# A decoder layer on one core: self attention's normalised rows are turned by VectorE and a DRAM round trip, the last tile's probabilities by TensorE, and two groups of loads are asked for by ScalarE's queue

## The chip, the cores and the metric

The kernel runs on one core of a Trainium2 chip. Its time is the device time of one execution in microseconds (us). TensorE is written PE in the profile, VectorE DVE, ScalarE ACT, GpSimd POOL, and SyncE SP; PEld is TensorE's loading of weights, which lies beside its matmuls.

## The reference, cut to what matters

A pre-norm decoder layer over x of 4 x 1024 rows of 512 numbers, in float32. Three parts are added to x one after the other: a self attention against 2048 given keys and values, a cross attention of 16 heads over 1601 context rows, and a mixture of experts. The change is in the first part alone:

```
def _L0_attn_ref(q, k, v, scale_factor, dropout_p):
    b, s, d = q.shape                      # 4, 1024, 512
    step = s // 4
    scale = q[:, ::step].reshape(b, -1)    # 4 normalised rows of a batch: 2048 numbers, one for each key
    qk = jnp.einsum('bsd,btd->bst', q, k)  # against 2048 keys
    scaled_qk = qk * scale[:, None, :]
    softmax_qk = jax.nn.softmax(scaled_qk, axis=-1)
    return jnp.einsum('bst,btv->bsv', softmax_qk, v)

x = x + _L0_attn_ref(_layernorm(x, axis=-1), L0_attn_k, L0_attn_v, L0_attn_scale_factor, L0_attn_dropout_p)
```

## The kernel before, in words

`self_attention` (line 97) writes one instruction stream for each engine by hand; semaphores order them, and no scheduler moves anything. It works on 32 tiles of 128 rows. Every number that goes into a matmul is split into a high and a low part, and a product is three matmuls of 512 columns (`matmul3`: lines 47 to 49, high by high, high by low, low by high). For tile t:

- VectorE makes the normalised rows (`normalize`, `sa_normed`, L498). Rows lie on partitions, but a matmul wants the 512 numbers of a row on partitions, so TensorE turns them by four 128x128 transposes (`turn`, `sa_nT_ps`, L322). ScalarE copies the high part (`high_n`, L417) and VectorE makes the low part (`low_n`, L503).
- TensorE scores the tile against four groups of 512 keys (`score`, 48 matmuls). VectorE multiplies by the scale (`scale_block`, L515; the trace calls the buffer `rows`, since it is a part of the `rows` tensor of the next stage), finds the maximum (`row_max`, L519), ScalarE takes the exponential (`exp`, L422).
- The probabilities have to be turned as well. VectorE turns all 32x32 squares in one instruction (`turn_p`, L523), SyncE sends the result to the DRAM tensor `turned_p` (L223), waits until it is there, and reads it back in four pieces, which puts the squares in their places (`move`, L226). ScalarE makes the high part (`high_p`, L430), GpSimd the low part (`low_p`, L291).
- TensorE weighs the values (`weigh`, 48 matmuls into `sa_o_ps`), and VectorE adds (`add`, L540).

TensorE's stream for tile t is: the scores of tile t+1, the turn of tile t+2, the weighing of tile t. So a tile's probabilities have one weighing and one scoring of other tiles to get through exponential, turning, DRAM and splitting. The exponential of tile t+1 writes the buffer from which `low_p(t)` reads, and waits for it. Tile 0's probabilities are turned by TensorE (`turn_first_p`, L348), as nothing is there to cover a trip.

The scale rows of the batches (1 MB each, `load_scale`, L219) and the three weights of the next stage (1 MB each, L255) are asked for by SyncE in its own order. The weights are turned by TensorE (`turn_last`, L373, into the banks of the scores, with ScalarE L439 and VectorE L575 splitting them) with three groups of context rows: 15 groups, nine of them before the last tile's weighing, one behind each quarter of it, and three at its end. The next stage begins with L878.

## Time and profile before

| | |
|---|---|
| median of 3 runs | 3819.49 us (3815.13 to 3820.21) |
| the profiled execution | 3817.16 us, of which the span is 3815.3 us |
| granted TensorE clock, mean | 0.993 |
| TensorE, VectorE, ScalarE, GpSimd busy | 98%, 63%, 38%, 44% |
| self attention | from the start to 769.67 us |

How to read it: times are microseconds from the span's start. "Busy" counts instructions from start to end; as TensorE's matmuls overlap (a row says 0.39 us where the next begins 0.23 us later), the distance between two starts says what a matmul costs, and its duration does not. A row of the timeline is: start, length of the row in us, engine, line, operation, what it writes <- what it reads, shape, count; in brackets the idle time of the engine before it and what ended it. PEclk is the granted TensorE clock as a share of 2.4 GHz. SPq rows are DMAs as SyncE asks for them.

### The profile page before, as it was taken

The numbers are of one execution on the slowest core, as the hardware profiler recorded it, in microseconds if no ns is written. First come the engines' busy times: TensorE is split into PE (matmuls) and PEld (weight loads), VectorE is DVE, ScalarE is ACT, GpSimd is POOL, SyncE is SP. The second block draws the span as 40 slices with busy tenths as digits, with TensorE's granted clock in tenths as the row PEclk, the third lists the DMA queues.
The fourth block names the chain that finished last, engine by engine and source line by source line (L and its number), as shares of the span: only waits on it lengthen the run. The fifth ranks groups of instructions, "written<-read, shape, count | busy, mean of one in ns | idle before, by whom it ended". The sixth has DMA issues, their size and how long they took to land. (4 is left out here: it accounts for less than half of the span.)

```text
span 3815.3 us, 62978 instructions
## 1 busy us (share of the span) xinstructions
PE 3730.7 (98%) x18664; PEld 2480.3 (65%) x18665; DVE 2386.6 (63%) x6129; ACT 1434.0 (38%) x1793; POOL 1687.6 (44%) x984
## 2 busy tenths in 40 slices
PE   8999999999988999999999999999999999999998
PEld 7888888788876544444444444454444777777886
DVE  6544444344466888888888888888888543434235
ACT  3222222222333455545555455545555221222332
POOL 2222222200023776677666766676665222312334
PEclk9999999999999999999999999999999999999999
DMA  6444444555565122222211222222211434327679
GB/s 203 125 128 131 134 121 121 162 199 187 180 196 180 36 58 58 58 56 58 58 29 34 58 58 59 58 56 58 48 31 40 157 123 138 111 89 257 213 279 340
DMA packets 245485, 446.75 MB, mean 117 GB/s; under 512 B 20024, under 2 KB 104536, under 8 KB 241244
## 3 DMA queue, kind: packets, MB, share of 16 engines
q1 hardware_dynamic: 215196, 366.37, 33.3%
q0 software_dynamic: 14752, 49.29, 3.6%
q10 hardware_dynamic: 15264, 27.79, 1.9%
q8 instruction: 130, 2.13, 0.2%
q14 instruction: 143, 1.17, 0.1%
HBM read 262.21 MB, written 181.17 MB: 116 GB/s over the span
## 5 line engine op out<-in xcount | busy, mean ns | idle before, releaser
L1165 DVE CUSTOM_DVE_ANT_0 xf_unread<-xa_mx_ps,mask_q 128x402 bf16<-128x402 f32 x1984 | 1033.7, 574 | 279.0 <-PE xa_mx_ps L1158 152.8
L1788 ACT ACTIVATE probs<-xa_scores 128x1024 f32<-128x1024 f32 (+1 forms) x416 | 417.5, 1024 | 417.6 <-PE xa_scores L1662 411.5
L1788 ACT ACTIVATE xa_probs<-xa_scores 128x1024 f32<-128x1024 f32 (+1 forms) x416 | 417.3, 1024 | 387.0 <-PE xa_scores L1662 387.0
L1662 PE MATMUL xa_scores<-mask_t,ident_b 128*128 128x512 bf16 (+1 forms) x1664 | 549.4, 388 | 0.0
L1623 POOL TENSOR_TENSOR xa_sums<-xa_sums,xa_probs 128x1024 f32<-128x1024 f32 x220 | 519.6, 2383 | 18.1 <-POOL xa_sums L1623 15.9
L1623 POOL TENSOR_TENSOR xa_sums<-xa_sums,probs 128x1024 f32<-128x1024 f32 x220 | 519.4, 2380 | 18.1 <-POOL xa_sums L1623 14.6
L1158 PE MATMUL xa_mx_ps<-xa_kp,queries 96*128 96x402 f32 x1024 | 364.7, 418 | 0.0
L1158 PE MATMUL xa_mx_ps<-xf_kp,queries 96*128 96x402 f32 x960 | 342.1, 418 | 0.0
L1656 PE MATMUL xa_scores<-queries,xf_kp 97*128 97x512 f32 (+1 forms) x832 | 284.7, 423 | 15.1 <-ACTq L1810 8.3
L1158 PEld LDWEIGHTS xa_mx_ps<-xa_kp,queries 96*128 96x128 f32 x1024 | 181.7, 189 | 169.4 <-DVE xf_maxima L1165 107.8
L1656 PE MATMUL xa_scores<-queries,xa_kp 97*128 97x512 f32 (+1 forms) x832 | 284.5, 423 | 1.8 <-ACT probs L1788 1.8
L1662 PEld LDWEIGHTS xa_scores<-mask_t,ident_b 128*128 128x128 bf16 (+1 forms) x1664 | 122.9, 100 | 244.5 <-issue 211.8
L1158 PEld LDWEIGHTS xa_mx_ps<-xf_kp,queries 96*128 96x128 f32 x960 | 170.3, 189 | 159.6 <-DVE xf_maxima L1165 102.2
L291 POOL TENSOR_TENSOR sa_pT_low<-rows,sa_pT_high 128x512 fp32r<-128x512 f32 x124 | 156.9, 1299 | 186.0 <-ACT sa_pT_high L430 186.0
L430 ACT ACTIVATE sa_pT_high<-rows 128x512 fp32r<-128x512 f32 x124 | 68.1, 621 | 406.2 <-DMA rows<-turned_p 406.2
L47 PE MATMUL sa_o_ps<-sa_v_high,sa_pT_high 128*128 128x512 f32 x512 | 203.7, 398 | 7.7 <-POOL sa_pT_low L291 7.3
L49 PE MATMUL sa_scores<-weights,sa_nT_low 128*128 128x512 f32 x512 | 204.3, 399 | 0.0
L47 PE MATMUL sa_scores<-weights,sa_nT_high 128*128 128x512 f32 x512 | 202.5, 395 | 1.4 <-DVE sa_nT_low L503 1.4
L48 PE MATMUL sa_scores<-queries,sa_nT_high 128*128 128x512 f32 x512 | 202.7, 396 | 0.0
L1656 PEld LDWEIGHTS xa_scores<-queries,xf_kp 97*128 97x128 f32 (+1 forms) x832 | 148.9, 187 | 82.4 <-ACT xa_probs L1788 26.0
L49 PE MATMUL sa_o_ps<-sa_v_high,sa_pT_low 128*128 128x512 f32 x512 | 200.3, 391 | 0.0
L48 PE MATMUL sa_o_ps<-sa_v_low,sa_pT_high 128*128 128x512 f32 x512 | 200.1, 391 | 0.0
(418 smaller groups left out, 7258.4 us busy)
## 6 DMA issues: line engine op xcount, KB each, us to landing
turned_p<-rows SPq DMA_DIRECT2D x31, 1024.0 KB, 3.8
rows<-turned_p SPq DMA_DIRECT2D x124, 256.0 KB, 4.6
bridge_rows<-sorted_in SPq DMA_DIRECT2D x78, 256.0 KB, 3.3
sorted_out<-ex_made ACTq DMA_DIRECT2D x78, 256.0 KB, 4.3
queries<-qT_high SPq DMA_DIRECT2D x30, 512.0 KB
xf_kp<-kT_high SPq DMA_DIRECT2D x16, 800.5 KB, 11.8
xa_kp<-kT_high SPq DMA_DIRECT2D x16, 800.5 KB
rows<-in_ctx SPq DMA_DIRECT2D x16, 768.0 KB, 4.8
```

Source lines behind the costliest of these rows:

```text
L47: pe.matmul(out, lh, rh, start=start, stop=False)
L48: pe.matmul(out, lh, rl, start=False, stop=False)
L49: return pe.matmul(out, ll, rh, start=False, stop=stop)
L291: pool.tensor_tensor(pT[1][:, mine, :].rearrange("p c (i q) -> p c i q", q=SQUARE), raw_pT[:, mine, :, :], words(pT[0][:, mine, :]).rearra ...
L430: act.activation(pT[0][:, mine, :].rearrange("p c (i q) -> p c i q", q=SQUARE), raw_pT[:, mine, :, :], ACT.Copy).then_inc(pT_high, 1)
L1158: return pe.matmul(out[:, 0:MKEYS], qp[0:MAXROW, j, first:first + P], kp[0:MAXROW, j, MFIRST[kb]:MFIRST[kb] + MKEYS], start=True, stop=True)
L1165: return dve.tensor_tensor_reduce(out=unread[slot % 2][:, :], in0=scores[:, 0:MKEYS], in1=mask_q[:, half * QB + qt, MFIRST[kb]:MFIRST[kb] ...
L1623: pool.tensor_tensor(sums[pr][:, :, :], left[pr][:, :, :], right[pr][:, :, :], ALU.add).then_inc(pool_added, 1)
L1656: pe.matmul(scores[pr][0:keys, jj, :], kp[par][0:ROWS97, j, kt * P:kt * P + keys], qp[par][0:ROWS97, j, queries], start=True, stop=False)
L1662: last = pe.matmul(scores[pr][0:keys, jj, :], ident_b[0:keys, 0:keys], mask_t[0:keys, kt, queries], start=False, stop=True)
L1788: act.activation(prob[ring][pr][0:keys, :, :], scores[pr][0:keys, :, :], ACT.Exp, scale=SCALE).then_inc(exped, 1)
```

## The change

Rows are turned in another way for tiles 2 to 31. VectorE turns the 32x32 squares of the normalised rows (`turn_n`, into `sa_spare`), SyncE sends them to a new DRAM tensor `turned_n` and reads them back in four pieces into `sa_normed` (`move_n`); ScalarE (`high_moved_n`) and VectorE (`low_moved_n`) split them from there. In the tile, both now stand behind the exponential and behind the turning of the probabilities. TensorE no longer turns rows in the tiles' loop. The last tile's probabilities are turned by TensorE, as the first tile's (`turn_end_p`), and the groups of `turn_last` are spread over its weighing, three behind each quarter. The scales of batches 1 to 3 and the three weights are asked for by ScalarE, one in each of tiles 0 to 2 and 26 to 28, behind that tile's exponential.

```
+                def move_n(t):
+                    sp.wait_ge(turned, t + 3)
+                    sp.dma_start(turned_n, spare[:, :]).then_inc(n_out, 16)
+                    sp.wait_ge(n_out, 16 * (t - 1))
+                    for a in range(QB):
+                        sp.dma_start(normed[a * SQUARE:(a + 1) * SQUARE, :].rearrange("k (i n) -> k i n", n=P),
+                                     turned_n[:, a * P:(a + 1) * P].rearrange("(i k) n -> k i n", k=SQUARE)).then_inc(n_in, 16)
...
-                load_scale(1)
-                for t in range(2):
-                    if t > 0:
+                def ask(t):
+                    if not (isinstance(t, int) and t == 0):
                         load_add(t)
                         store(t - 1)
                     load_norm(t + 3)
+                    move_n(t + 2)
                     move(t + 1)
-                    load_scale(t + 2)
...
-                sp.wait_ge(scaled_to, NB * (tiles - S // P) + NB + 1)
-                for w, weight in enumerate(weights):
-                    sp.dma_start(scale[:, w, :, :], weight.rearrange("(r p) n -> p r n", p=P)).then_inc(weights_in[w], 16)
...
                 def tile(t, ahead):
-                    first = isinstance(t, int) and t == 0
-                    for j in range(NB) if ahead >= 1 else ():
-                        if first and j == NB - 1:
-                            turn_first_p(0)
-                            turn_first_p(1)
+                    ends = isinstance(t, int) and t in (0, tiles - 1)
+                    for j in range(NB - 1) if ahead >= 1 else ():
                         score(t + 1, j)
-                    if ahead >= 2:
-                        turn(t + 2)
-                    for n in range(AHEAD) if ahead == 0 else ():
-                        turn_last(n)
+                    for j in range(2) if ends else ():
+                        turn_end_p(t, j)
+                    if ahead >= 1:
+                        score(t + 1, NB - 1)
                     for j in range(NB):
                         weigh(t, j)
-                        if first and j + 2 < NB:
-                            turn_first_p(j + 2)
-                        if ahead == 0 and AHEAD + j < GROUPS_W:
-                            turn_last(AHEAD + j)
+                        if ends and j + 2 < NB:
+                            turn_end_p(t, j + 2)
+                        for n in range(FULL) if ahead == 0 else ():
+                            turn_last(FULL * j + n)
...
+                def high_moved_n(t):
+                    act.wait_ge(scored, NB * t)
+                    act.wait_ge(n_in, 16 * QB * (t - 1))
+                    act.activation(nT[0][:, :, :].rearrange("p c (i r) -> p c i r", r=SQUARE), raw_nT,
+                                   ACT.Copy).then_inc(nT_high, 1)
+
...
+                def load_weight(w):
+                    act.wait_ge(scaled_to, NB * (tiles - S // P) + NB + 1)
+                    act.dma_start(scale[:, w, :, :],
+                                  weights[w].rearrange("(r p) n -> p r n", p=P)).then_inc(weights_in[w], 16)
...
                     if ahead >= 1:
                         exp(t + 1)
+                    if isinstance(t, int) and t < B - 1:
+                        if t == 0:
+                            wait_v_split(act)
+                        load_scale(t + 1)
+                    if isinstance(t, int) and 0 <= t - WEIGHTS_FROM < len(weights):
+                        load_weight(t - WEIGHTS_FROM)
+                    if ahead >= 2:
+                        high_moved_n(t + 2)
...
+                def turn_n(t):
+                    dve.wait_ge(normal, t + 3)
+                    if isinstance(t, int) and t == 2:
+                        dve.wait_ge(v_low_pool, POOL_V)
+                    else:
+                        dve.wait_ge(n_out, 16 * (t - 2))
+                    dve.transpose(n_squares, normed_by_row).then_inc(turned, 1)
+
...
                     invert(t)
                     if ahead >= 2:
                         normalize(t + 2)
+                        turn_n(t + 2)
...
+                    for j in range(2, NB) if ends else ():
+                        low_end_p(t, j)
+                        for n in range(FULL) if ahead == 0 else ():
+                            low_last(FULL * (j - 2) + n)
+                    if ahead >= 1 and not (isinstance(t, int) and t + 1 == tiles - 1):
+                        turn_p(t + 1)
                     if ahead >= 2:
-                        low_n(t + 2)
+                        low_moved_n(t + 2)
```

On VectorE the loop over tiles read so before, from the tile's rows being normalised (L498) to the sum of the tile before (L540):

```order
L498 TENSOR_SCALAR sa_normed<-sa_x_norm,sa_mean_var,sa_rstd 128x512
L515 TENSOR_TENSOR rows<-sa_scores,sa_scale 128x512
...
L519 TENSOR_REDUCE sa_neg_max<-rows 128x1
L503 TENSOR_TENSOR sa_nT_low<-sa_nT_ps,sa_nT_high 128x512
L523 STREAM_TRANSPOSE rows<-rows 128x2048
L540 SCALAR_TENSOR_TENSOR sa_out<-sa_o_ps,sa_inv_total,sa_x_add 128x512
```

The same place of the changed kernel (its lines are numbered anew):

```order
L525 TENSOR_SCALAR sa_normed<-sa_x_norm,sa_mean_var,sa_rstd 128x512
L534 STREAM_TRANSPOSE sa_spare<-sa_normed 128x512
L556 TENSOR_TENSOR rows<-sa_scores,sa_scale 128x512
...
L560 TENSOR_REDUCE sa_neg_max<-rows 128x1
L564 STREAM_TRANSPOSE rows<-rows 128x2048
L542 TENSOR_TENSOR sa_nT_low<-sa_normed,sa_nT_high 128x512
L581 SCALAR_TENSOR_TENSOR sa_out<-sa_o_ps,sa_inv_total,sa_x_add 128x512
```

A transpose of 128x512 has come in ahead of the first scaling, and the low part of the rows has gone behind the turning of the probabilities. SyncE's queue in the same loop is now:

```order
L208 DMA sa_x_add<-in_x 128x512
L212 DMA x<-sa_out 128x512
...
L204 DMA sa_x_norm<-in_x 128x512
L232 DMA turned_n<-sa_spare 128x512
L235 DMA sa_normed<-turned_n 32x4x128 x4
...
L224 DMA turned_p<-rows 128x2048
L227 DMA rows<-turned_p 32x4x512 x4
```

L232 and L235 are new; the others stand in the order that they had.

## Rows read from the trace of the kernel before

**Rows 1.** The page: busy time of each engine.

```profile
PE 3730.7 (98%) x18664; PEld 2480.3 (65%) x18665; DVE 2386.6 (63%) x6129; ACT 1434.0 (38%) x1793; POOL 1687.6 (44%) x984
```

**Rows 2.** Stretches: us, then each engine's busy time, PEclk, DMA share, GB/s.

```profile
0.00:769.67 769.67, 747.61 (x3341) 609.76 (x3342) 379.53 (x510) 183.80 (x272) 191.19 (x180) 0.99 0.46 140
...
70.00:75.00 5.00, 3.41 (x17) 2.63 (x16) 3.59 (x4) 2.67 (x5) 2.97 (x3) 1.00 1.04 357
...
750.00:752.00 2.00, 2.00 (x7) 1.52 (x6) 0.00 (x0) 0.00 (x0) 2.00 (x2) 0.50 0.00 0
```

**Rows 3.** Waits of TensorE to 770 us: in total, times, longest.

```profile
PE sa_o_ps L47 <- POOL sa_pT_low L291: 7.3, 2, 5.7
...
PE cxl_banks L878 <- SPq L843: 3.3, 1, 3.3
```

**Rows 4.** Timeline of TensorE, the last loop tile and the tile behind the loop.

```profile
693.31 0.40 PE L47 MATMUL sa_scores<-weights,sa_nT_high 128*128 128x512 f32 x1
...
704.52 0.60 PE L322 MATMUL sa_nT_ps<-ident,sa_normed 128*128 128x128 f32 x4
...
705.18 0.39 PE L48 MATMUL sa_o_ps<-sa_v_low,sa_pT_high 128*128 128x512 f32 x1
...
715.86 0.40 PE L47 MATMUL sa_scores<-weights,sa_nT_high 128*128 128x512 f32 x1
...
727.08 0.40 PE L47 MATMUL sa_o_ps<-sa_v_high,sa_pT_high 128*128 128x512 f32 x1
...
738.00 1.25 PE L373 MATMUL sa_scores<-ident,sa_scale 128*128 128x128 f32 x10
```

**Rows 5.** Timeline of the other engines, one trip of the probabilities in the loop.

```profile
599.58 0.32 SPq L223 DMA_DIRECT2D turned_p<-rows  x1
603.43 1.74 SPq L226 DMA_DIRECT2D rows<-turned_p  x4
...
603.48 0.75 DVE L540 SCALAR_TENSOR_TENSOR sa_out<-sa_o_ps,sa_inv_total,sa_x_add 128x512 f32<-128x512 f32 x1 [3.93 <-PE sa_o_ps L49]
...
606.40 0.55 DVE L498 TENSOR_SCALAR sa_normed<-sa_x_norm,sa_mean_var,sa_rstd 128x512 f32<-128x512 f32 x1 [0.67 <-POOL sa_rstd L281]
...
607.12 0.34 SPq L200 DMA_DIRECT2D sa_x_norm<-in_x  x1
...
610.37 2.20 ACT L430 ACTIVATE sa_pT_high<-rows 128x512 fp32r<-128x512 f32 x4 [13.17 <-DMA rows<-turned_p]
...
611.09 5.04 POOL L291 TENSOR_TENSOR sa_pT_low<-rows,sa_pT_high 128x512 fp32r<-128x512 f32 x4 [4.72 <-ACT sa_pT_high L430]
...
617.66 2.01 ACT L422 ACTIVATE rows<-rows,sa_neg_max 128x2048 f32<-128x2048 f32 x1 [2.12 <-DVE sa_neg_max L519]
...
619.79 2.31 DVE L523 STREAM_TRANSPOSE rows<-rows 128x2048 f32<-128x2048 f32 x1 [1.56 <-ACT rows L422]
...
622.13 0.32 SPq L223 DMA_DIRECT2D turned_p<-rows  x1
```

**Rows 6.** Timeline of SyncE and ScalarE, returns of two later tiles.

```profile
693.64 1.75 SPq L226 DMA_DIRECT2D rows<-turned_p  x4
...
696.59 0.91 SPq L255 DMA_DIRECT2D sa_scale<-in_L_xattn_Wq_w  x1
...
700.86 2.20 ACT L430 ACTIVATE sa_pT_high<-rows 128x512 fp32r<-128x512 f32 x4 [13.44 <-DMA rows<-turned_p]
...
716.19 1.74 SPq L226 DMA_DIRECT2D rows<-turned_p  x4
...
724.09 2.20 ACT L430 ACTIVATE sa_pT_high<-rows 128x512 fp32r<-128x512 f32 x4 [14.12 <-DMA rows<-turned_p]
```

**Rows 7.** Timeline of tiles 0 and 1.

```profile
47.22 1.28 DVE L527 TENSOR_TENSOR sa_pT_low<-sa_k_ps,sa_pT_high 128x512 fp32r<-128x512 f32 x2
...
48.05 0.47 PE L47 MATMUL sa_o_ps<-sa_v_high,sa_pT_high 128*128 128x512 f32 x1 [0.35 <-DVE sa_pT_low L527]
...
56.05 2.01 ACT L422 ACTIVATE rows<-rows,sa_neg_max 128x2048 f32<-128x2048 f32 x1 [0.76 <-DVE sa_pT_low L527]
...
58.18 2.31 DVE L523 STREAM_TRANSPOSE rows<-rows 128x2048 f32<-128x2048 f32 x1 [2.16 <-ACT rows L422]
...
59.96 0.40 PE L47 MATMUL sa_scores<-weights,sa_nT_high 128*128 128x512 f32 x1
...
73.36 0.50 PE L47 MATMUL sa_o_ps<-sa_v_high,sa_pT_high 128*128 128x512 f32 x1 [1.59 <-POOL sa_pT_low L291]
```

**Rows 8.** Timeline of the last tile.

```profile
748.85 0.76 PE L47 MATMUL sa_o_ps<-sa_v_high,sa_pT_high 128*128 128x512 f32 x1 [5.72 <-POOL sa_pT_low L291]
749.41 0.63 PE L48 MATMUL sa_o_ps<-sa_v_low,sa_pT_high 128*128 128x512 f32 x1
...
763.50 0.60 PE L373 MATMUL sa_scores<-ident,rows 128*128 128x128 f32 x4
...
764.37 3.67 DVE L575 TENSOR_TENSOR queries<-sa_scores,queries 128x512 fp32r<-128x512 f32 x6
...
769.67 1.09 PE L878 MATMUL cxl_banks<-ident,rows 128*128 128x128 f32 x4 [3.31 <-SPq L843]
```

135 lines of the change are left out of this document (71 added, 64 removed).

## The prediction

> **What bounds the kernel now.** The page comes first: TensorE is busy 98% of the span, VectorE 63% [rows 1]. The stretches tell where the change acts: self attention takes the first 769.67 us, and TensorE is busy in 747.6 of them, so at most 22 us are rest and the others are matmuls [rows 2]. The waits say what the rest is: two waits for the low part of the probabilities, 7.3 us, one of them 5.7; the other long one is the entry to the next stage, 3.3 us [rows 3]. In the loop over tiles there is none. So in the loop only TensorE's own work can be saved, and at the two ends waits can.
>
> The timeline of TensorE gives the price of its work. A tile of the loop runs from 693.31 to 715.86, 22.55 us: 11.21 of scores, then the four transposes and the weighing. The next tile has no rows to turn any more and takes 22.14 us (11.22 and 10.92) [rows 4]. It is the control that the trace holds by itself: a turn costs 22.55 - 22.14 = 0.41 us, and the new loop tile is this tile.
>
> Then I read the other engines, to see whether they can follow at 22.14. From one exponential to the next the probabilities go: exponential and turning by VectorE 4.47 us (617.66 to 622.13), out to DRAM 3.85 (599.58 to 603.43), back 6.94 (to 610.37), first high part to first low part 0.72, four low parts 5.04; together 21.02 us [rows 5]. The slowest return took 7.90, which makes 21.98 [rows 6]. Both are below 22.14, the second by little.
>
> **The change part by part.**
>
> *The turn leaves TensorE.* 30 turns stood in the tiles (rows of tiles 2 to 31). The first two lie ahead of the weighing of tile 1, whose start is set by the probabilities (below), so 28 count: 28 x 0.41 = 11.5 us.
>
> The Trainium skill, "VectorE: DVE Perf Modes", The three transpose paths, gives 390 ns for a 128x128 bf16 transpose on TensorE and advises TensorE for it where PSUM is a fit target; by it alone a turn would be worth an estimated 4 x 0.39 = 1.56 us, 44 us in all, or the change a step to the wrong engine. The trace disagrees with that price as a price in a stream: there the four cost 0.41 together, as they overlap their neighbours.
>
> *What the rows now do.* They are normalised at 606.95 [rows 5]. VectorE turns 512 columns in 2.31 / 4 = 0.58 us, to 607.6; SyncE has asked for the next rows at 607.12 and is free. The way out and back of 0.25 MB was never run; its lower end is nothing beyond the asking, the upper end is what the 1 MB of the probabilities took, 3.85 + 6.94, which gives 618.4. ScalarE reaches the copy after the exponential, at 619.9. So the rows are there even by the upper end. The copy takes 0.55 (a quarter of 2.20), VectorE does its part behind the turning, 622.1 to 622.8, and the scores that need it begin a new period after 603.1, at 625.2. 2.4 us are spare. The 0.58 on VectorE moves the first scaling from 606.9 to 607.5, and VectorE has room: it works 379.5 of the 769.67 us [rows 2]. I take 0 for all of it. It costs something once the rows come back later than 623.9, 16 us after they were asked for.
>
> *What the loop's probabilities lose.* Between the end of a tile's scores and its own weighing stood two turns, which both go, so their cover shrinks by 0.8. The first low part is there at 611.09 + 1.3 = 612.4; the weighing's place is four periods of 22.55 ahead of 704.9, 614.7. The 2.3 us spare become 1.5, and 0.5 with the slowest return. I take no wait. The new DMAs stand behind the return in SyncE's queue. What a queue behind it does is shown: with the three weights, 3 MB, asked for right behind (696.59), the return took 7.22 in place of 6.94 [rows 6].
>
> *The scales and weights on ScalarE's queue.* Two queues at work at once were not seen in this stage. 1 MB takes 2.9 us at the 357 GB/s of the busiest stretch [rows 2]. It is asked for at the end of the exponential, 2.3 us ahead of the probabilities' way out, so they overlap by about half a microsecond; none and 2.9 are the ends. I take 0.5 at the start, and 0 at tiles 26 to 28, where 1.5 us are spare. The weights also leave SyncE's queue, where nothing waited for them.
>
> *The first tiles.* Ahead of tile 0's weighing VectorE now turns rows (0.6) before three scalings and the first low part. That part is what the weighing waited for (0.35 at 48.05), so it begins at 48.65 and the turn that TensorE saved is lost. It ends 11.9 later at 60.6. The exponential of tile 1 starts at 56.65 for 56.05, the turning of its probabilities ends at 61.1, and only then comes the low part of tile 2's rows, 61.8: TensorE waits 1.3 us, a new wait. But the weighing of tile 1 waits for probabilities in any case: 73.36 + 0.6 + 0.5 = 74.5 [rows 7]. The scores before it end at 61.9 + 11.2 = 73.1. So the start costs +1.1 us, with 0.6 and 3.5 as ends. Afterwards the trip of 21 us has the period of 22.14 to catch up.
>
> *The last tile.* Before: nine groups of weights 5.13 us (738.00 to 743.13), the wait of 5.72, the weighing with four groups 14.65 (748.85 to 763.50), and 6.17 to the next stage's first matmul [rows 4, 8]. In the weighing the first matmuls stand 0.42 us apart for 0.23, at a granted clock of 0.50, 1.2 GHz: after the rest of 5.7 us TensorE ran at half speed [rows 2, 8]. Now the probabilities are turned in place. The first quarter needs one turn 0.41, ScalarE 0.55, VectorE 0.61 (3.67 / 6) and the handing over, about 2.0 in all; then 10.92 for the weighing, two more turns 0.82, nine groups 3.7: 17.4 us against 25.5. The tail is as before, since six groups and the sum are still left for VectorE there (0.75 + 3.67). 8.1 us less. Bounds: 5.7 (only the wait goes) and 9.
>
> *The sum.* -11.5 + 1.1 - 8.1 = -18.5 us against the profiled execution's 3817.16 (span 3815.3 and 1.9 around it): 3798.7. That execution is 2.3 below the median of the runs, 3819.49. The four times known average 3818.0, and from there the sum gives 3799.5; I forecast 3800.
>
> **The rivals.**
>
> *Two queues share the DMA engines fully.* Then every 1 MB pushes the way out by 2.9: start +3.5 in place of 1.1, and a trip of 23.9 against 22.14 for two more tiles, +3.5; at tiles 26 to 28 first 1.4, then twice 1.8, 5.0. The sum becomes -18.5 + 2.4 + 3.5 + 5.0 = -7.6, about 3810. For it: in the start the queue was full (1.04 share, rows 2) when a load met a return. Against: the load has a start of 2.3 us. The Trainium skill, "DMA: Bandwidth & Descriptors", Issuing engines are not separate DMA queues, says that DMAs of all engines run on the same 16 DMA engines and interleave. The trace of before can't show it here, since all came from SyncE.
>
> *The trip becomes the period.* Rows out and back are 0.5 MB more a tile, 1.4 us at 357 GB/s. If they all fall on the probabilities, 21.02 becomes 22.42, 0.28 above 22.14, 28 x 0.28 = 8 us: 3808; with slower returns mixed in 0.4 a tile, 3811. Against: they are asked for at 607.7, when the return is nearly in (610.37), and end long before 622.13.
>
> *Slower than before.* The same trip, from the point where it takes over 22.14 + 18.5 / 28 = 22.8 us. If the added 1.4 came on top of the slowest return, 23.4, each tile would wait 1.24: +35 - 18.5 = +16, about 3834. The one return of 7.90 among normal ones speaks for a trip that stretches now and then; that it did so in few tiles is against it.
>
> *The clock.* If TensorE's rest of about 1.2 us ahead of the last weighing let the clock fall as the rest of 5.7 did, 11 matmuls cost 0.2 more, and perhaps all 48: +2 to +9, near 3806. Against: at 73.36 it had rested 1.59 us, and the clock in that stretch was 1.00 [rows 2, 7].
>
> *Rows too late*, past 623.9, is a case with the trip: the queue that delays one delays both.
>
> **How the numbers follow.** Forecast 0.64. Full sharing of the queues 0.12 (3810). The trip as the period 0.13 (3808 to 3813), half of it still faster. Slower than before 0.05. The clock 0.04 (3806). Better than the sum 0.02. A measurement of this kernel can tell about 0.2%, 7.6 us, from no change; the bound is 3810.4 from 3818. Faster: 0.64 + 0.12 + 0.065 + 0.04 + 0.02, about 0.88; within 0.07; slower 0.05. The forecast's own range is 3796 to 3805 (the bounds of start and end, and the runs' spread of 2.5 to either side); for 8 in 10 it reaches to 3809.
>
> **What would show it.** In the changed kernel the loop tile must be 22.1 us from scores to scores, with no wait in it; the turning of rows on VectorE about 0.6 us; the rows back before ScalarE has done the exponential; the returns of the probabilities near 7 us, and slower in tiles 1 to 3 and 27 to 29 if the queues share. The wait of 5.7 us and the 1.2 GHz behind it must be gone, and the stage must end near 751 us. The forecast is wrong if the loop tile stays at 22.4 or above, if a wait for the rows stands in it, or if the last tile from the end of weighing 30 to the next stage takes over 27 us.

## The result

The changed kernel takes 3807.89 us (median of 9 runs, 3804.34 to 3813.48), the kernel before 3819.79 (9 runs, 3815.13 to 3824.26): ratio 0.9973, 95% interval 0.9963 to 0.9983. It is 11.9 us, 0.3%, faster (the ratio goes by the means, which are 10.3 apart). The forecast was 3800, with an own range of 3796 to 3805 and a wider one, for 8 in 10, up to 3809; 18.5 us were to go. The median lies outside the forecast's own range, inside the wider one, and a third of the gain is missing. The profiled execution of the changed kernel took 3806.69, of which 3804.8 are the span.

The page, busy time of each engine, answers to [rows 1]:

```profile
PE 3723.5 (98%) x18560; PEld 2469.3 (65%) x18561; DVE 2408.7 (63%) x6162; ACT 1430.9 (38%) x1793; POOL 1682.1 (44%) x980
```

The stretches answer to [rows 2]; the first row of each kernel ends at the first matmul of the next stage, the second runs to the end. The changed kernel:

```profile
0.00:753.25 753.25, 733.58 (x3236) 596.25 (x3238) 400.15 (x543) 180.83 (x272) 186.11 (x176) 1.00 0.53 161
753.25:3804.80 3051.55, 2989.89 (x15324) 1873.10 (x15324) 2008.59 (x5619) 1250.10 (x1521) 1496.04 (x804) 0.99 0.37 111
```

and the second stretch of the kernel before, which is new here:

```profile
769.67:3815.30 3045.63, 2983.14 (x15324) 1870.57 (x15324) 2007.05 (x5619) 1250.17 (x1521) 1496.38 (x804) 0.99 0.37 111
```

Self attention ends at 753.25 in place of 769.67, 16.4 us earlier. Behind it stands the same program in both, with the same 15324 matmuls, and it takes 3051.55 in place of 3045.63 us: 5.9 of the 16.4 are given back there. So there are two questions, whether the 16.4 came about as forecast, and where the 5.9 went. The first can be read from the trace, the second needed the experiments.

**The loop.** TensorE's timeline, one tile from scores to scores, answers to [rows 4]:

```profile
594.76 0.40 PE L47 MATMUL sa_scores<-weights,sa_nT_high 128*128 128x512 f32 x1
...
616.90 0.40 PE L47 MATMUL sa_scores<-weights,sa_nT_high 128*128 128x512 f32 x1
```

594.76 to 616.90 is 22.14 us, as the control tile of [rows 4] had it, and no wait stands in it. The other engines, one trip, answer to [rows 5] (SyncE, then ScalarE, then VectorE):

```profile
591.67 0.34 SPq L224 DMA_DIRECT2D turned_p<-rows  x1
595.54 1.73 SPq L227 DMA_DIRECT2D rows<-turned_p  x4
...
599.50 0.33 SPq L232 DMA_DIRECT2D turned_n<-sa_spare  x1
605.05 1.74 SPq L235 DMA_DIRECT2D sa_normed<-turned_n  x4
...
602.61 2.20 ACT L438 ACTIVATE sa_pT_high<-rows 128x512 fp32r<-128x512 f32 x4 [12.79 <-DMA rows<-turned_p]
609.34 2.01 ACT L430 ACTIVATE rows<-rows,sa_neg_max 128x2048 f32<-128x2048 f32 x1 [4.53 <-DVE sa_neg_max L560]
...
611.34 0.62 ACT L424 ACTIVATE sa_nT_high<-sa_normed 128x512 fp32r<-128x512 f32 x1
...
598.76 0.71 DVE L534 STREAM_TRANSPOSE sa_spare<-sa_normed 128x512 f32<-128x512 f32 x1
...
611.47 2.31 DVE L564 STREAM_TRANSPOSE rows<-rows 128x2048 f32<-128x2048 f32 x1 [2.16 <-ACT rows L430]
613.70 0.65 DVE L542 TENSOR_TENSOR sa_nT_low<-sa_normed,sa_nT_high 128x512 fp32r<-128x512 f32 x1
```

The rows leave at 599.50 and are asked back at 605.05. Out they take 5.55 us, more than the 1 MB of the probabilities with 3.87; the return of the probabilities, which ends at 602.61, and three other requests are under way ahead of them. The exponential ends at 611.3 and ScalarE copies them at once, so they were back in time. VectorE turns them in 0.71 us (0.58 was worked out). The probabilities come back in 602.61 - 595.54 = 7.07.

**The waits** to the end of self attention answer to [rows 3]:

```profile
PE cxl_banks L922 <- SPq L887: 3.3, 1, 3.3
PE sa_o_ps L47 <- DVE sa_pT_low L568: 2.6, 2, 1.5
PE sa_o_ps L47 <- POOL sa_pT_low L297: 2.4, 2, 1.5
...
PE sa_scores L47 <- DVE sa_nT_low L542: 1.1, 1, 1.1
```

Of the 5.7 us ahead of the last weighing 1.1 are left (the row with 2.6; its other wait is tile 0's, 1.5 us for 0.35 before). New is the wait of 1.1 for the rows of tile 2, as forecast; of the 2.4 for the probabilities 1.5 stand in tile 1 and 0.84 ahead of tile 30's weighing (717.64 in the rows of the last tile), which was not forecast. Tile 30's probabilities take 5.36 us on the way out (702.40 to 707.76) in place of 3.87, and 7.75 back. In every profile where a packet of TensorE's own instructions (explained with e12 below) starts within 0.5 us of the request for this way out, it takes 5.1 to 5.5 us; in the kernel before, e3, e12, e14, e16 and e18, which have none there, 3.9.

**The start** answers to [rows 7] (TensorE, ScalarE with its queue, SyncE, ScalarE):

```profile
48.31 0.47 PE L47 MATMUL sa_o_ps<-sa_v_high,sa_pT_high 128*128 128x512 f32 x1 [1.50 <-DVE sa_pT_low L568]
...
61.50 0.49 PE L47 MATMUL sa_scores<-weights,sa_nT_high 128*128 128x512 f32 x1 [1.09 <-DVE sa_nT_low L542]
...
74.48 0.50 PE L47 MATMUL sa_o_ps<-sa_v_high,sa_pT_high 128*128 128x512 f32 x1 [1.52 <-POOL sa_pT_low L297]
...
56.34 2.01 ACT L430 ACTIVATE rows<-rows,sa_neg_max 128x2048 f32<-128x2048 f32 x1 [0.76 <-DVE sa_pT_low L568]
56.40 0.44 ACTq L448 DMA_DIRECT2D sa_scale<-in_x  x1
...
64.69 1.73 SPq L227 DMA_DIRECT2D rows<-turned_p  x4
...
72.45 2.19 ACT L438 ACTIVATE sa_pT_high<-rows 128x512 fp32r<-128x512 f32 x4 [13.50 <-DMA rows<-turned_p]
```

The weighing of tile 1 starts at 74.48, 1.12 later than before (+1.1 was forecast). The number is right by luck: SyncE asks for the return at 64.69, 0.31 later than before (64.38; 0.6 was forecast for VectorE's new turn), and the return takes 7.76 us, 0.81 more than before (64.38 to 71.32; 0.5 was forecast for the load beside it). One assumption was wrong: ScalarE's request for the scales was put at the end of the exponential. It is issued at 56.40, when the exponential starts. The requests run ahead of the engine's own work, and the load then meets the probabilities' way.

**The last tile** answers to [rows 8]:

```profile
717.64 0.47 PE L47 MATMUL sa_o_ps<-sa_v_high,sa_pT_high 128*128 128x512 f32 x1 [0.84 <-POOL sa_pT_low L297]
...
728.63 1.03 PE L353 MATMUL sa_k_ps<-ident,rows 128*128 128x128 f32 x8
730.79 0.47 PE L47 MATMUL sa_o_ps<-sa_v_high,sa_pT_high 128*128 128x512 f32 x1 [1.13 <-DVE sa_pT_low L568]
...
746.71 1.47 PE L378 MATMUL sa_scores<-ident,sa_scale 128*128 128x128 f32 x12
748.02 1.96 PE L378 MATMUL sa_scores<-ident,rows 128*128 128x128 f32 x12
753.25 0.63 PE L922 MATMUL cxl_banks<-ident,rows 128*128 128x128 f32 x4 [3.28 <-SPq L887]
```

From the end of weighing 30 (728.63) to the next stage 24.62 us; before it was 769.67 - 738.00 = 31.67. So 7.05 us less, for 8.1 forecast. The clock stays at its upper level, 2.4 GHz: in the last tile the granted clock is 1.00.

Together: +1.1 at the start, 664.64 - 654.15 = 10.5 less between the starts of weighing 1 and the end of weighing 30, 7.05 at the end: 16.4.

### The profile page after: what moved, and what is told of

Read it like the earlier page. It is cut to its first block and busy times, and to the rows that moved or that the text cites. A ratio compares the mean times of both kernels' runs of the same rounds, so it can differ in the third digit from the quotient of the medians.

```text
span 3804.8 us, 62828 instructions
## 1 busy us (share of the span) xinstructions
PE 3723.5 (98%) x18560; PEld 2469.3 (65%) x18561; DVE 2408.7 (63%) x6162; ACT 1430.9 (38%) x1793; POOL 1682.1 (44%) x980
## 6 DMA issues: line engine op xcount, KB each, us to landing
xf_kp<-kT_high SPq DMA_DIRECT2D x16, 800.5 KB, 11.8
```

## The experiments

Every kernel ran in turns with the kernel before on the same chip, and only differences to that are compared further: beside e4b to e7 the kernel before took 3831 us, beside e16 to e18 3834, beside the others 3819 to 3821. The table gathers what the texts below use. "Matmuls ahead" is how many more matmuls than before stand in TensorE's program ahead of the loop of the cross attention; this loop has six rounds, and "round" is a fifth of the time from its first to its last start. "Late load" is the time from SyncE's last request for the late weights, near 3120 us, to ScalarE's use of them. "To before" is median less median; the interval of the ratio goes by the means.

| kernel | matmuls ahead | self attention ends | round | late load | to before | ratio |
|---|---|---|---|---|---|---|
| before | 0 | 769.67 | 215.9 | 3.0 | | |
| before, e8 | 0 | 772.38 | 216.0 | 3.1 | -1.9 | 0.9987 to 1.0005 |
| e1 place | 0 | 771.38 | 216.1 | 3.1 | +0.6 | 0.9992 to 1.0010 |
| e3 ends | +16 | 762.15 | 216.9 | 2.8 | -2.3 | 0.9991 to 1.0022 |
| e2 rows | -8 | 761.46 | 215.6 | 3.1 | -11.4 | 0.9958 to 0.9981 |
| e9 rows | -8 | 761.32 | 215.9 | 3.2 | -11.8 | 0.9959 to 0.9979 |
| e16 rows, 16 transposes | +8 | 762.43 | 215.7 | 3.9 | -7.3 | 0.9972 to 0.9990 |
| e17 rows, tile 30 in loop | -104 | 761.52 | 218.6 | 2.9 | +4.7 | 1.0004 to 1.0022 |
| changed | +8 | 753.25 | 216.1 | 4.9 | -11.9 | 0.9963 to 0.9983 |
| changed, e7 | +8 | 754.60 | 216.3 | 4.6 | -13.5 | 0.9957 to 0.9981 |
| changed, e15 | +8 | 753.45 | 216.3 | 4.8 | -13.0 | 0.9955 to 0.9979 |
| e10 context | +8 | 753.30 | 216.5 | 4.4 | -12.5 | 0.9955 to 0.9978 |
| e4b loads | +8 | 752.37 | 216.2 | 4.9 | -9.8 | 0.9961 to 0.9982 |
| e6 rest | +8 | 763.03 | 216.2 | 4.4 | -1.4 | 0.9986 to 1.0004 |
| e11 work, 40 | +48 | 755.40 | 219.8 | 3.0 | +7.3 | 1.0011 to 1.0029 |
| e5 work, 80 | +88 | 760.78 | 224.4 | 2.9 | +40.4 | 1.0094 to 1.0125 |
| e12 front, 80 | +88 | 762.03 | 224.5 | 3.0 | +43.0 | 1.0096 to 1.0127 |
| e13 front, 120 | +128 | 763.21 | 216.2 | 3.0 | -3.4 | 0.9981 to 0.9999 |
| e14 fold | -88 | 753.81 | 216.3 | 3.0 | -15.7 | 0.9947 to 0.9974 |
| e14 fold, e18 | -88 | 754.15 | 216.5 | 3.1 | -13.2 | 0.9947 to 0.9975 |

**e1, the DRAM tensor alone.**

```
-    turned_p = dram("turned_p", [P, T1 // BANK, BANK])
+    turned_p, turned_n = dram("turned_p", [P, T1 // BANK, BANK]), dram("turned_n", [P, D])
```

> The kernel before, with one DRAM tensor of 0.25 MB more (the place for the turned rows), which nothing uses; it moves the addresses of the DRAM tensors allocated behind it. Theory P (place): the 5.9 us that the changed kernel lost behind self attention (3051.55 us from the next stage's first matmul to the end, against 3045.63) come from where the later tensors lie. Then self attention ends at 769.7 as before, the part behind it takes about 3051, and the ratio is 1.0012 to 1.0016. Theory C (chance and phase): that part varies by some us from program to program for its own waits and clock drops, whatever the addresses. Then the ratio is within 0.9995 to 1.0005.

The ratio is 1.0001: where the later tensors lie costs nothing. Its self attention ended at 771.38, and in e8 at 772.38. So the 769.67 of the first profile was the luckiest of three (mean 771.1; the changed kernel's three average 753.8), and the change takes off about 17.4, not 16.4. What is given back is 4 to 6 us by the medians, from 11.9 to 13.5 gained, and 5 to 7 by the means.

**e2 and e9, rows without the new last tile.** The last tile is as before: `low_p(tiles - 1)` on GpSimd, `move(t + 1)` for it, its groups ahead of the weighing.

```
-        ends = isinstance(t, int) and t in (0, tiles - 1)
+        ends = isinstance(t, int) and t == 0
```

> The changed kernel with the last tile as before: its probabilities go through DRAM again, the weights' nine groups stand ahead of its weighing; rows and loads stay changed. Theory of the prediction's sum, with the sizes that the trace of the changed kernel showed: rows give 10.5 us in the loop, the start costs 1.1, the last tile gives nothing, self attention ends at 760.3. If what is lost behind self attention (5.9 us) comes with the rows (tensor, queue), the time is 3.5 us below before (ratio 0.9991); if it hangs on when the stage ends or is chance, the ratio is 0.9975 to 0.9985. Rival: the last tile's wait is longer here than the 5.7 us of before, since nothing else hides the return of the probabilities and tile 30's weighing ends earlier by the turns that are gone: stage end at 762 or later.

> The changed kernel with the last tile as before, once more, on one chip with the kernel before and the next one. The first time it was 11.4 us faster than before, with self attention ending at 761.5, 8 us ahead of 769.7. Plain sum: 8 to 10 us faster than before (ratio 0.9974 to 0.9979), and 6 to 8 us slower than the next one. Rival: again as fast as the kernel with the new last tile, so that the new last tile is worth nothing in the time.

Self attention ends at 761.4, 1.1 later than worked out (the last tile's wait is 5.3 us in e2, not longer), and the time is 11.4 and 11.8 below before: all that the whole change gained. The stage gains 771.1 - 761.4 = 9.7, so nothing of it is given back; e9's rival, as fast as the whole change, came true.

**e3, the new last tile alone.** The other half of the diff on the kernel before.

> The kernel before with the last tile alone changed: its probabilities are turned by TensorE in place and the weights' groups stand between the quarters of its weighing. Rows are still turned by TensorE, the loads are asked for by SyncE. Theory of the sum: the last section is 7.1 us shorter, self attention ends at 762.6, and the time is 7 us below before (ratio 0.9982) if nothing is given back later; if a stage end that comes earlier gives back a third of it (as 5.9 of 16.4 in the changed kernel), 4.5 us (0.9988). The granted clock stays 1.00 in the last weighing. Rival: the wait of 5.7 us moves to the first quarter's turning and the section gains under 4 us, with the clock at 0.5 for a while: stage end at 766 or later.

The stage ends at 762.15, 7.5 us earlier than in the first profile of before and 9.0 than the mean of three, and the time is 2.3 below before, not distinguishable from none. Three of its twelve runs took 3836 to 3840; they were not explained. The two halves together: the rows bring what they bring in their stage, the new last tile brings some 8 us in its stage and nothing in the time that can be told from none.

**e7, e5 and e6: is a later end made up?** e7 is the changed kernel again. e5 has work ahead of the last weighing (first two lines), e6 has rest there (the others):

```
+                    for n in range(80) if ahead == 0 else ():
+                        pe.transpose(nT_ps[:, n % DC, :], ident[:, :], ident[:, :])
...
+                    for n in range(3) if t > 0 and j == 0 else ():
+                        act.activation(pT[0][:, :, :].rearrange("p (j c) q -> p j (c q)", c=KB), prob[:, :, :], ACT.Copy)
+                        act.drain()
```

> The changed kernel once more, for a second profile and more runs beside the three kernels below. So far the kernel without the new last tile was as fast as the whole change (3808.4 against 3807.9), though its self attention ended 8.2 us later. Theory G (given back behind): the new last tile gains its 7 to 8 us in self attention and the stages behind give them back; then self attention ends at 753 +- 1 again, the part behind it takes 3050 to 3053 us, and the time is 3806 to 3809. Theory N (noise of the runs): the part behind it takes 3045 to 3048 in this profile, and the time comes out at 3800 to 3804.

> The changed kernel with 80 more transposes of the identity, which nothing uses, on TensorE ahead of the last weighing: 80 x 0.103 us = 8.2 us of work, of which 1.1 us lie in the wait that stands there. Self attention ends about 7 us later, near 760, with TensorE busy all the time. Theory D (the stages behind hang on when they begin, and a later begin is made up): the time is 0 to 3 us above the changed kernel. Theory R (it is rest that they make up, since TensorE after a rest is granted its full clock more often later): busy work is not made up, the time is 6 to 8 us above the changed kernel. Plain sum: 7 us above.

> The changed kernel with three more copies of the probabilities on ScalarE (2.2 us each, their values are overwritten) ahead of the first high part of the last tile: TensorE rests some 6.7 us more ahead of the last weighing, and should be granted 1.2 GHz for a while behind it, as in the kernel before (5.7 us of rest, 7.4 us at 1.2 GHz). Self attention ends 7 to 10 us later, 760 to 763. Theory R: the rest is made up behind self attention, the part behind it takes 3045 to 3048 us and the time is 0 to 3 us above the changed kernel. Theory D: the same by the later begin alone, and the kernel with the added transposes shows it too. Plain sum: 7 to 10 us above the changed kernel.

e7 is 13.5 us faster than before, with self attention ending at 754.60; the part behind it takes 3059.1 us here, where before is slower too. Neither a later end nor rest is made up: e6 ends the stage 8.4 us after e7 and takes 12.1 more. Its wait of 7.1 (row below) brought the half clock back, as forecast (granted 0.50 from 736 to 742 us). Both theories fall.

```profile
PE sa_o_ps L47 <- DVE sa_pT_low L571: 7.1, 1, 7.1
```

e5 was the surprise. Its self attention ends at 760.78, as worked out, but it takes 53.9 us more than e7. TensorE's waits over the whole program say where:

```profile
PE xa_o_ps L1716 <- issue: 32.0, 6, 6.3
...
PE xa_scores L1702 <- issue: 6.5, 6, 1.4
```

"issue" is time in which TensorE waited for nothing that the profile shows. No other kernel so far had the first row. One of the six, in the timeline:

```profile
2117.34 0.72 PE L1702 MATMUL xa_scores<-queries,xf_kp 97*128 97x512 f32 x2 [1.38 <-issue]
...
2125.77 1.94 PE L1716 MATMUL xa_o_ps<-probs,xf_vg 128*32 128x512 f32 x8 [6.35 <-issue]
```

Each ends at one place of the cross attention's loop, some seven us behind the start of a round; the first comes 700 us behind the edit, the last 1800. So an instruction in self attention can cost time in a loop that it has nothing to do with. That gave the theory of the place.

**e4b, the loads on SyncE's queue.**

```
+                    sp.dma_start(scale[:, b, :, :], rows_of_scale[b].partition_broadcast(P)).then_inc(scale_in[b % 2], 16)
 ...
-                    act.dma_start(scale[:, b, :, :], rows_of_scale[b].partition_broadcast(P)).then_inc(scale_in[b % 2], 16)
```

> The changed kernel with the scales and the weights asked for by SyncE's queue in the old places; rows and last tile stay changed. Theory L: ScalarE's requests, which are issued when the exponential starts, share the DMA engines with the way out and the return of the probabilities, and cost about 1 us in the first tiles (returns of 7.8 and 8.0 us in tiles 1 and 2, a wait of 2.0 us in tile 2). Without them the returns are 6.9 to 7.3, the wait of tile 2 is under 1 us, and self attention ends at 752 to 752.5 against 753.25. Rival N: the start is set by the later low part of tile 2's rows and by VectorE's added turn, and the loads change nothing or make it worse, since on one queue each load stands ahead of a way out: stage end at 753.3 or later, up to 757. In time both are within 0.1% of the changed kernel.

Theory L held in the stage. SyncE asks for the scales behind the return, which then takes 71.13 - 64.17 = 6.96 us; with ScalarE's request it took 72.45 - 64.69 = 7.76 (rows of the start above). The wait shrinks from 1.52 to 0.70:

```profile
64.17 1.73 SPq L227 DMA_DIRECT2D rows<-turned_p  x4
65.94 0.43 SPq L257 DMA_DIRECT2D sa_scale<-in_x  x1
...
71.13 2.19 ACT L446 ACTIVATE sa_pT_high<-rows 128x512 fp32r<-128x512 f32 x4 [12.67 <-DMA rows<-turned_p]
...
73.17 0.49 PE L47 MATMUL sa_o_ps<-sa_v_high,sa_pT_high 128*128 128x512 f32 x1 [0.70 <-POOL sa_pT_low L305]
```

So the two queues share, at a price of 0.8 us for 1 MB; the forecast had put 0.5, its rival 2.9. The Trainium skill, "DMA: Bandwidth & Descriptors", Issuing engines are not separate DMA queues, says that they interleave on the same engines; the trace agrees. In the time nothing of it was seen: this kernel is 3.7 us slower than e7, intervals overlapping.

**e8 and e10: clock, or the queue at the stage's end?** e10 is one wait: `sp.wait_ge(pT_low, NB * tiles + NB)` in place of `sp.wait_ge(k_turned, T1C + 2 * NB)`.

> The kernel before, as a run of its own, for a second profile of it. In the profiles so far, the part behind self attention splits into TensorE's waits (48 to 51 us, 59 to 64 us on another chip), the time lost at the granted clock of 0.5 (12 to 20 us) and a rest that is the same in all (2982 to 2986 us). Theory K (clock): the 5.9 us that the changed kernel lost there in the first pair of profiles are stretches at half clock that the first profile of before happened to miss (12.3 us lost against 14 to 20 in all others); this profile then shows 14 to 18 us lost and 3047 to 3052 us behind self attention. Rival W (waits): the changed kernel waits more there because of what it does; then this profile shows 3045 to 3047 again, with 12 us lost.

> The changed kernel with one wait of SyncE as before: the second half of the next stage's rows is asked for when the last low part of the last tile is done, and no more when TensorE has turned its last quarter, some 6 us earlier. Theory Q (queue): the earlier request is what costs behind self attention (bridge parts 5.8 us of waits before, 8.4 with the change); then the time is 3 to 5 us below the changed kernel's, 16 us below before (ratio 0.9957). Rival: nothing, ratio 0.9963 to 0.9972 as the changed kernel had it, and self attention ends at 753 to 754, since the rows are still there in time.

e8 lost only 9.9 us to the half clock behind self attention, and yet took 3049.1 there, with waits of 54.0: neither theory as put. What it says is how wide chance is: the kernel before took 3045.6, 3047.6 (e1) and 3049.1 behind self attention. e10 is where the changed kernel is (-12.5): the earlier request costs nothing, theory Q falls.

**e11, e12, e13: place or amount?** e11 has 40 of e5's transposes, e12 and e13 have 80 and 120 at the start of TensorE's program:

```
+                for n in range(80):
+                    pe.transpose(nT_ps[:, n % DC, :], ident[:, :], ident[:, :])
                 for i in range(KB):
                     turn_k(i)
```

> The changed kernel with 40 unused transposes ahead of the last weighing (the run before had 80). With 80 self attention ended at 760.8, as worked out, but TensorE then stood six times for 5.3 us, released by nothing (issue), at one place of the loop of the cross attention, 220 us apart, each with a stretch at half clock behind it: 54 us in all. Theory I (the place of the instructions): what costs is where the loop's instructions come to lie, not how many there are; 40 more put them elsewhere, the six stalls are gone (at most 1.2 us each at the loop's start, as always), self attention ends at 756 to 757, and the time is 3 us above the changed kernel's. Rival S (the amount): half the transposes, half the stalls or the time: some 16 us of stalls, and 20 to 30 us above the changed kernel.

> The changed kernel with the 80 unused transposes at the very start of TensorE's program, where it waits 5.6 us for the first keys, and no more ahead of the last weighing. In the profiles the period of the cross attention's loop (six rounds, 1300 us behind this place) goes with the number of matmuls that stand in TensorE's program ahead of it: 8 fewer than in the kernel before 215.6 to 215.9 us, as before 215.9 to 216.1, 8 more (the changed kernel) 216.1 to 216.5, 16 more 216.9, 48 more 219.8, 88 more 224.4. Theory P (place): only how far the loop's instructions are pushed counts, so 88 more at another point of the program give the same: six stalls of about 5 us released by nothing, a period near 224, and 45 to 55 us above the changed kernel. Rival T (timing at the end of self attention, or what the transposes did there): the period is 216.1 to 216.5 and the time 4 to 6 us above the changed kernel. Self attention ends at 758 to 760 in either.

> The changed kernel with 120 unused transposes at the start of TensorE's program, 128 matmuls more ahead of the loop of the cross attention than in the kernel before. Theory P (place in a repeating block): if the stretch of instructions after which the pattern repeats holds 128 matmuls or a part of that, the period is 216 us again and the time is 8 to 10 us above the changed kernel (the added work: 120 x 0.103 = 12.4, less 3 to 4 in the wait for the first keys). Theory A (the more stands ahead, the worse): the period is 228 us or more, 6 x 12 us and more above the changed kernel. Between them, a longer block that has not come round yet looks like A.

e11 refutes theory I as it was put (the round is 219.8, not 216), and looked like the amount. e12 and e13 decide. The same 80 at another point give the same round, 224.5, and the same row:

```profile
PE xa_o_ps L1716 <- issue: 34.9, 6, 6.5
```

And 128 matmuls ahead give 216.2 again: e13 takes 9.6 us more than e15, and its self attention ends 9.8 later, so all of it is the added work. Not how many instructions stand ahead counts, but where the loop's come to lie. Two stretches of e12, at the start of a round, show what it meets (columns as in [rows 2]):

```profile
2120.00:2124.00 4.00, 2.10 (x8) 0.91 (x8) 0.00 (x0) 2.05 (x3) 1.00 (x1) 1.00 0.99 237
2124.00:2128.00 4.00, 0.00 (x0) 0.00 (x0) 0.00 (x0) 0.00 (x0) 3.64 (x2) 0.91 1.01 201
```

The DMA engines are full (0.99 and 1.01): SyncE loads the next group's keys and values. In the changed kernel they are as full at the same point, and TensorE works on:

```profile
2084.00:2088.00 4.00, 2.89 (x20) 1.07 (x16) 0.00 (x0) 2.19 (x3) 0.49 (x1) 1.00 0.88 224
2088.00:2092.00 4.00, 4.00 (x23) 2.30 (x23) 3.03 (x11) 2.09 (x3) 4.00 (x2) 1.00 1.03 204
```

So a full queue alone does no harm. The trace's DMA records tell what ends the stalls. Queue q8 carries instructions in packets of 16384 bytes, and in these kernels its number of packets (the first figure of the page's line) changes only with edits of TensorE's program: 130 in the kernel before and in the changed one, 137 in e5 and e12, 136 in e11, e14, e17 and e18, 131 in e13. The lines of the changed kernel and of e12:

```profile
q8 instruction: 130, 2.13, 0.2%
q8 instruction: 137, 2.24, 0.3%
```

In the stall that ends at 2129.12 in e12, one such packet starts at 2126.10 and ends at 2127.46, and TensorE goes on 1.66 us later. In all twelve stalls of e5 and e12 a packet ends 1.4 to 1.7 us before TensorE goes on. In e12 these packets start 4.0 to 5.7 us behind the first matmul of a round. In the changed kernel one starts there too, at 3.8 to 4.5 us, but TensorE has work meanwhile. So TensorE stands for its own instructions, which come through DMA while the engines are full of loads. That the packet has to wait behind the loads is inferred: the trace tells when it starts, not when it was asked for. The Trainium skill, "Runtime: NRT & Kernel Launch", Instruction fetch mechanics, says that a sequencer fetches its instructions by its own DMA queue in blocks of 256 instructions, 16 KiB, mostly hidden, and that a branch can force a fetch. The packets of 16384 bytes agree with the blocks. By it 128 matmuls with their weight loads are one block, and e13 would lie as before; its round of 216.2 and its one packet more agree. But -88 and -104 against +48 and +88 don't follow such a period simply: e14 has one packet more in each round, as e12 has, and loses nothing by it. Which places are bad stays open.

**e14, e15 and e18, tile 30 in the loop.** Since TensorE turns no rows any more, tile 30 has the same instructions as those before it.

```
-                with pe.Fori(0, tiles - 3) as t:
-                    tile(t + 1, 2)
-                tile(tiles - 2, 1)
+                with pe.Fori(0, tiles - 2) as t:
+                    tile(t + 1, 1)
```

> The changed kernel with tile 30 taken into the loop over tiles on TensorE: since the rows are no longer turned there, its instructions are the same as those of the tiles before. 96 matmuls fewer stand in the program, 88 fewer than in the kernel before. Nothing changes in self attention, which ends at 753 to 755. Theory A (the fewer stand ahead, the better): the loop of the cross attention has its period of 215.6 or less in place of 216.1 to 216.5, so 3 us or more come back, time 3 us or more below the changed kernel's (ratio to before 0.996 or below). Theory P with a block of 128 matmuls: 88 fewer are 40 more, the period is about 219, and the kernel is 15 to 18 us slower than the changed one. Theory N (numbers by chance): the time stays within 1 us of the changed kernel's.

> The changed kernel as it is, beside the three above on one chip, for their comparison: 10 to 14 us faster than before (ratio 0.9963 to 0.9973), self attention ends at 753 to 755, the period of the cross attention's loop is 216.0 to 216.5 us. If the period is 215.9 or below, the differences of half a microsecond between the kernels with 8 matmuls fewer or more are chance.

> The changed kernel with tile 30 taken into TensorE's loop, once more: 14 to 17 us faster than before (ratio 0.9955 to 0.9963), self attention ends at 753 to 754, no wait near 3125 us. The part behind self attention takes 3046 to 3049 us, against 3050 to 3052 in the changed kernel's profiles.

e14 and e15 differ on TensorE's program alone. Their stages end at 753.81 and 753.45, their medians are 3802.86 and 3805.62. The rounds are equal (216.3), so theory A's reason is wrong, but one difference is exact. In e15 the late weights land late, and TensorE waits for them and falls to 1.2 GHz (SyncE, ScalarE, TensorE, and the stretch):

```profile
3116.08 0.34 SPq L2241 DMA_DIRECT2D hdl_late_raw<-in_L_ffn_w_shared_out  x1
...
3120.84 0.63 ACT L2418 ACTIVATE ws_high<-hdl_late_raw 128x512 fp32r<-128x512 f32 x1 [1.83 <-DMA hdl_late_raw<-in_L_ffn_w_shared_out]
...
3126.35 0.83 PE L2324 MATMUL bridge_ps<-ident,bridge_part 128*128 128x128 f32 x4 [1.88 <-DVE queries L2518]
```

```profile
3126.00:3130.00 4.00, 3.65 (x12) 3.02 (x13) 2.23 (x9) 0.60 (x1) 1.72 (x2) 0.58 0.11 43
```

In e14 they are there in 3.0 us, and there is neither the wait nor the half clock:

```profile
3115.15 0.34 SPq L2240 DMA_DIRECT2D hdl_late_raw<-in_L_ffn_w_shared_out  x1
...
3118.17 0.63 ACT L2417 ACTIVATE ws_high<-hdl_late_raw 128x512 fp32r<-128x512 f32 x1
```

```profile
3122.00:3130.00 8.00, 7.86 (x38) 6.15 (x37) 3.57 (x10) 1.09 (x2) 2.90 (x3) 1.00 0.18 67
```

In the table, the load takes 3.9 to 4.9 us in all seven profiles with 8 matmuls more ahead, and 2.8 to 3.2 in all thirteen others, whatever else they change. The DMA records have the reason here as well: in these seven a packet of q8 starts 1.1 to 1.3 us after the request and runs beside the load, for 1.1 us in e16 (load 3.9) and 2.2 in the changed kernel (load 4.9); of the thirteen others only e3 has one in the load's time, from 0.3 to 1.2 us behind the request, and its load takes 2.8. Whether e14 is really the faster one can't be told: the intervals of its ratio (0.9960 and 0.9961 in e14 and e18) overlap with those of the changed kernel.

**e16 and e17, the place without the new last tile.** e16 is e2 with 16 transposes at the start, e17 is e2 with e14's loop.

> The kernel with rows and loads changed and the last tile as before (3808.4 and 3808.9 in two calls, as fast as the whole change) with 16 unused transposes at the start of TensorE's program, in the wait for the first keys. It has then as many matmuls ahead of the later loops as the changed kernel has, 8 more than before in place of 8 fewer. Theory P (place): what the changed kernel loses behind self attention comes with those 16; then the time goes up by 3 to 6 us (3812 to 3815 where before is 3819), the wait of TensorE for the part of the late weights near 3125 us (1.6 to 2.0 us in every profile with 8 more, 0.3 or none in the others) stands there, and the period of the cross attention's loop is 216.1 to 216.5. Rival L (the new last tile itself): the time stays 11 to 12 us below before, without that wait.

> Rows and loads changed, last tile as before, and tile 30 taken into TensorE's loop (104 matmuls fewer ahead of the later loops than before). With the next kernel it is the pair that has old and new last tile at places that are both free of the stalls. Self attention ends at 761 to 762. Theory P: the last tile is worth in the time what it is worth in self attention, so this kernel is 7 to 8 us slower than the next one, 8 to 9 us faster than before (ratio 0.9977). Rival L: 0 to 3 us slower than the next one, since the new last tile gives its gain back wherever the instructions lie.

e16 goes from -11.6 (e2, e9) to -7.3: 16 matmuls more ahead cost this kernel some 4 us, of which 1.0 stands in self attention itself (762.43 for 761.4), with the late load at 3.9 and a wait of 1.0 for it. The intervals overlap (0.9972 to 0.9990 against 0.9958 to 0.9981 and 0.9959 to 0.9979), so this is likely and not shown. Its rounds take 215.7, so the small differences between 215.6 and 216.5 are not by the place. Against the changed kernel at the same place (-11.9 to -13.5) the new last tile is worth 4.6 to 6.2 us after all, median less median. e17 was to be a place without stalls and is not: its rounds take 218.6 us, 6 x 2.6 us more, with half clock behind five of them (each start stands for 2.4 to 2.7 us, elsewhere for 0.9 to 1.6). The pair with e18 tells nothing on the last tile, and it shows that good places can't be had by counting.

## Why the prediction was wrong

By its own steps:

- *The turn leaves TensorE*, 28 x 0.41 = 11.5. Right: the loop tile is 22.14 without a wait. 10.5 arrived, since 0.84 went into a wait at tile 30. The estimate of 44 us from the 390 ns in the Trainium skill, "VectorE: DVE Perf Modes", The three transpose paths, does not agree with that; the trace's own control tile was the right price.
- *What the rows do*, 0. Right: they are back before the exponential ends; the scores begin without a wait in the loop.
- *The probabilities' trip*, no wait. Right in the loop, with returns of 6.9 to 8.0 us and one of 8.5, but not at tile 30, with a wait of 0.84. The rival that the trip becomes the period did not happen; that its 3808 lies beside the measured time is chance, and so it is with the 3806 of the clock.
- *The loads on ScalarE's queue*, 0.5 at the start. Measured 0.8 by e4b. The mechanism was right, the time of the request was not: it is issued when the exponential starts. Full sharing (2.9) did not happen.
- *The first tiles*, +1.1. Measured +1.12, of which the terms were 0.6 and 0.5 and came out at 0.3 and 0.8: two errors cancel.
- *The last tile*, -8.1. Measured -7.05 in the stage: the weighing starts 2.16 us behind the one before (2.0 worked out), the part with turns and groups takes 0.5 more, the tail 0.4 more. The clock held. (Before, three groups stood in the last weighing, not four, one behind each of its first three quarters; no term hangs on it.)
- *The sum*, -18.5. In self attention -16.4 in the pair of profiles, about -17.4 against the mean of three profiles of before.
- *From the sum to the time.* This step failed. It was never written as one: the sum for a stage of 770 us was taken from the whole 3817, as if the 3045 us behind it could not change. They gave back 4 to 6 us. The 8.4 us between 3799.5, the sum's result, and the measured 3807.89 are 1.8 for the base (3818.0, where nine runs of before have 3819.79), 1.1 for the stage and 5.5 given back. Of what is given back, shown: the late load's wait, 1.7 to 2.0 us in the three profiles of the changed kernel and 0.3 or less where a packet of instructions does not fall on the load, with some 1.5 us more in two of them, where the clock falls behind it. Likely: that 16 unused transposes ahead cost the kernel with the old last tile 3 us behind the stage (e2, e9 against e16, on different chips, with overlapping intervals). In e3 the rounds are 1 us longer, 6 in all, but they don't explain its median: its profiled execution, the fastest of twelve, has them too and takes 3047.2 us behind self attention, as the kernel before does (3045.6 to 3049.1). Its first matmuls of the first and of the sixth round:

```profile
1445.11 0.50 PE L1660 MATMUL xa_scores<-queries,xf_kp 97*128 97x512 f32 x1 [1.07 <-issue]
...
2529.74 0.49 PE L1660 MATMUL xa_scores<-queries,xf_kp 97*128 97x512 f32 x1 [1.02 <-issue]
```

and of the changed kernel, 1080.3 us apart for 1084.6:

```profile
1437.08 0.50 PE L1700 MATMUL xa_scores<-queries,xf_kp 97*128 97x512 f32 x1 [1.02 <-issue]
...
2517.35 0.49 PE L1700 MATMUL xa_scores<-queries,xf_kp 97*128 97x512 f32 x1 [1.04 <-issue]
```

In the first pair of profiles the 5.9 split as waits 50.0 and 50.6, and stretches at half clock that cost 12.3 and 17.2 (summed over windows of 2 us, busy time x missing clock): three such stretches, at 1074, 2924 and 3126 us, stand in the changed kernel alone. Other profiles of the same two kernels have 9.9 (e8), 14.9 (e7) and 14.1 (e15). So much of what the pair shows is where the clock happened to fall, and only the medians show that 4 to 6 us are lasting.

Not settled: what the lasting part consists of beyond the late load (some 1 to 3 us), and at which places a packet of instructions comes too late. None of the rivals said it; all looked inside self attention.

## What to carry to other kernels

A gain in one stage is worth its full size only if what follows is left where it was, and an edit of the same engine's program moves all its later instructions, and with them the moments at which they are fetched by DMA. Where a long kernel has loops that start in a burst of loads, measure a change at two places (some unused instructions at the start, where the engine waits anyway) before it is believed or dropped: here 80 unused transposes cost some 47 us by their place, and 120 nothing by it. And let the forecast of a 0.5% gain hold a term for the untouched part, from the spread of that part between profiles of one kernel (3045.6 to 3049.1 here), 3 us or more to either side.

## What the runs showed of the hardware

- Six stalls of 4.4 to 6.5 us with no releaser, at one point of a loop, with 88 matmuls more ahead of it, wherever they stand; none with 48 or 128 more (at 48 the start of five of six rounds stands for 2.4 to 2.7 us, at 104 fewer that of all six).
- TensorE's instructions come in DMA packets of 16384 bytes on queue q8 (130 to 137 packets in these kernels). TensorE went on 1.4 to 1.7 us after a packet had ended, in all twelve stalls of e5 and e12, and a load of 256 KB landed in 3.9 to 4.9 us with such a packet beside it, in 2.8 to 3.2 without.
- DMA requests of ScalarE are issued while its previous instruction runs: 56.40 for an exponential from 56.34 to 58.35.
- The kernel before took 3819 to 3821 us beside some kernels, 3831 and 3834 beside others. The record gives the same chip, number 6, to the 3831 and to a 3821, so the chip alone is not the reason; in the profiles taken beside the slower ones TensorE waited 59 to 64 us behind self attention, for 48 to 56 elsewhere (kernels with stalls left out).
